# Self-attention: the output product's bias moves from a TensorE matmul to a GpSimd addition on the reloaded residual

## What is computed

```
x = x + cross_attention(layernorm(x), ctx, ctx, ...)
x = x + self_attention(layernorm(x), Wq, bq, Wk, bk, Wv, bv, Wo, bo)
x = x + experts(layernorm(x), ...)

self_attention:  q, k, v = x @ Wq.T + bq, x @ Wk.T + bk, x @ Wv.T + bv
                 q, k = rope(q), rope(k)
                 out = softmax(q k^T * scale) v
                 return out @ Wo.T + bo
```

## Time and profile before

| | |
|---|---|
| runs (median; lowest to highest) | 2096.05 us; 2095.18 to 2098.99 |
| profiled execution | 2098.95 us |
| its span, first to last instruction | 2097.2 us |
| mean granted TensorE clock | 0.992 |
| TensorE busy | 2041.1 us, 97% |
| VectorE, ScalarE, GpSimd busy | 1500.3, 1237.5, 998.9 us |
| self-attention: first normalisation, last store | 1323.7 us, 1582.9 us |

### The profile page before, as it was taken

The page is one execution under the profiler, slowest core; times in us unless marked ns, Lnnn a source line. Parts: engine busy times, 40 slices in busy tenths (PEclk is TensorE's granted clock), DMA queues, the critical chain, the costliest instruction groups (busy, mean ns, idle before and its releaser), DMA issues.

```text
span 2097.2 us, 48240 instructions
## 1 busy us (share of the span) xinstructions
PE 2041.1 (97%) x16424; PEld 1804.3 (86%) x16425; DVE 1500.3 (72%) x2690; ACT 1237.5 (59%) x3015; POOL 998.9 (48%) x835
## 2 busy tenths in 40 slices
PE   7999999999999999999999999899998999999997
PEld 6898988898899898889889988688877888888886
DVE  6667767767767767767667676799986877666665
ACT  4656666666666656656566565477773445555553
POOL 6433333333433333333343343488883334777775
PEclk9999999999999999999999999999999999999999
DMA  4000000000010010010010001255533222333332
GB/s 159 11 21 27 24 20 25 25 20 25 10 35 25 10 35 20 15 35 15 20 35 15 20 11 33 83 159 161 162 107 100 86 76 46 54 54 53 55 55 41
DMA packets 99645, 103.89 MB, mean 50 GB/s; under 512 B 10912, under 2 KB 89120, under 8 KB 99584
## 3 DMA queue, kind: packets, MB, share of 16 engines
q1 hardware_dynamic: 85952, 84.47, 12.9%
q0 software_dynamic: 13632, 18.62, 5.5%
HBM read 72.52 MB, written 30.54 MB: 49 GB/s over the span
## 4 chain that ended last, share of the span: by engine, by line
PE 75%; POOL 9%; issue 6%; DVE 4%; DMA 3%; ACT 2%; POOLq 0%; SPq 0%; DVEq 0%; ACTq 0%
PE banks L971 43%; PE banks L1077 5%; PE banks L1062 5%; PE banks L1026 4%; POOL out_dram L2505 4%; PE banks L1746 3%; POOL index L2476 3%; DMA out_dram<-r_y,index 2%; PE banks L2344 2%; POOL r_x L2469 2%; PE banks L1809 1%; PE banks L1768 1%; PE banks L1008 1%; PE banks L1825 1%; PE banks L2364 1%
## 5 line engine op out<-in xcount | busy, mean ns | idle before, releaser
L458 POOL TENSOR_TENSOR rinv<-rsum,inverse 128x4 f32<-128x4 f32 x112 | 112.9, 1008 | 482.9 <-ACT probs L593 482.9
L971 PE MATMUL banks<-ctxT_hi,qk_hi 128*128 128x256 f32 x1024 | 300.7, 294 | 0.0
L971 PE MATMUL banks<-ctxT_hi,qk_lo 128*128 128x256 f32 x1024 | 288.9, 282 | 0.0
L593 ACT ACTIVATE probs<-banks,nbias 128x256 f32<-128x256 f32 x512 | 236.8, 487 | 87.6 <-DVE nbias L736 87.6
L971 PE MATMUL banks<-ctxT_lo,qk_hi 128*128 128x256 f32 x1024 | 288.2, 281 | 0.0
L600 ACT ACTIVATE pc<-banks 128x512 f32<-128x512 f32 x256 | 155.7, 609 | 223.3 <-PE banks L971 223.3
L685 DVE TENSOR_TENSOR pT_lo<-banks,pT_hi 128x512 fp32r<-128x512 f32 x256 | 164.7, 685 | 111.3 <-ACT pT_hi L543 110.6
L731 DVE TENSOR_REDUCE peak<-banks 128x4 f32<-128x1024 f32 x128 | 156.6, 1224 | 122.4 <-PE banks L971 122.4
L461 POOL TENSOR_TENSOR probs<-probs,rinv 128x1024 f32<-128x1024 f32 x112 | 212.3, 1896 | 20.0 <-POOL rinv L458 20.0
L971 PE MATMUL banks<-pT_hi,ctx_hi 128*128 128x512 f32 x512 | 207.5, 405 | 3.2 <-DVE pT_lo L685 1.7
L971 PE MATMUL banks<-pT_hi,ctx_lo 128*128 128x512 f32 x512 | 202.0, 394 | 0.0
(11 more groups left out here) (282 smaller groups left out, 6106.2 us busy)
## 6 DMA issues: line engine op xcount, KB each, us to landing
ctx_raw<-in_ctx_dram SPq DMA_DIRECT2D x64, 256.0 KB, 2.7
experts_w<-in_L_ffn_We_dram SPq DMA_DIRECT2D x24, 512.0 KB, 4.0
x_in<-in_x_dram SPq DMA_DIRECT2D x16, 256.0 KB, 2.8
x_again<-in_x_dram SPq DMA_DIRECT2D x16, 256.0 KB, 2.8
x_stream<-z SPq DMA_DIRECT2D x16, 256.0 KB, 2.2
s_x<-x_stream SPq DMA_DIRECT2D x32, 128.0 KB, 3.8
s_x_again<-x_stream SPq DMA_DIRECT2D x32, 128.0 KB, 3.1
x_normalised<-s_xl SPq DMA_DIRECT2D x32, 128.0 KB, 1.7
```

Of the source, the lines that this page charges most:

```text
L458: nc.gpsimd.tensor_tensor(rinv[:, s % 2, :], rsum[:, s % 2, :], inverse[:, :], ALU.pow).then_inc(rinv_done, 1)
L593: nc.scalar.activation(probs[:, s % 2, p, :], scores[:, s % 2, p // 2, (p % 2) * SK:(p % 2 + 1) * SK], ACT.Exp, bias=nbias[:, s % 2, p:p + ...
L971: last = nc.tensor.matmul(out, a, b, start=(n == 0), stop=(n == 3 * len(pairs) - 1))
```

## The change

- TensorE no longer issues the matmul that brings bo into y (one 128x128 by 128x256 matmul with its weight load for each of 32 tiles); the first product with Wo opens the sum instead.
- GpSimd gets a new last part of its half-step: behind the multiplication of the probabilities of tile n it waits for the reload of x1_again of tile n-1, adds the float32 bias row to it in place (128x256), and counts up the new semaphore `x1_biased`.
- VectorE's addition of x2 waits for `x1_biased` where it waited for the reload: in half-step n it adds tile n-2 and needs the count n-1, which GpSimd reaches in its half-step n-1.
- The semaphores `pool_past` and `dve_past`, which nothing waits on, become one, `past`. The number of their increments is the same.

```diff
--- before.py
+++ after.py
@@ -1339,7 +1339,7 @@
     weights_in = sem("weights_in")
     small_in = sem("small_in")
     pool_setup = sem("pool_setup")
-    pool_past = sem("pool_past")
+    past = sem("past")
     bias_hi = sem("bias_hi")
     bias_done = sem("bias_done")
     setup_T = sem("setup_T")
@@ -1365,7 +1365,7 @@
     x3T_stored = [sem(f"x3T_stored{i}") for i in range(2)]
     dve_step = sem("dve_step")
     pool_step = sem("pool_step")
-    dve_past = sem("dve_past")
+    x1_biased = sem("x1_biased")
 
     bank_turns = [Turns(lambda kind, k=k: [key for key in pair_order(kind) if bank_of(key) == k],
                         -2, NT // 2 + 1, 4, STEADY) for k in range(SRING)]
@@ -1496,7 +1496,7 @@
             which = slice(0 if first else 1, 2 if second else 1)
             nc.gpsimd.tensor_tensor(rstd[:, which], mv[:, which, 1], power[:, which], ALU.pow).then_inc(rstd_done, 1)
             pool.wait_ge(rstd_done, g.tile(s, 4))
-            pool.sem_inc(pool_past, 1)
+            pool.sem_inc(past, 1)
 
     def normalised(out, src, which):
         return nc.gpsimd.tensor_scalar(out, src, mv[:, which, 0:1], rstd[:, which:which + 1],
@@ -1521,13 +1521,17 @@
                 pool.wait_ge(xl_stored[s], 16 * g.at)
                 key, pairs_on = before(g, s, ("x3T", s))
                 wait_filled(pool, g, key, pairs_on)
-            pool.sem_inc(pool_past, 1)
+            pool.sem_inc(past, 1)
             normalised(xl[:, s, :], x2[:, s, :], 1).then_inc(l3_done, 1)
         if g.has(s, 0):
             pool.wait_ge(rinv_done, g.tile(s, 1))
             heads = probs[:, s, :].rearrange("p (h k) -> p h k", k=SQ)
             nc.gpsimd.tensor_tensor(heads, heads, rinv[:, :].unsqueeze(2).broadcast_to([P, SH, SQ]),
                                     ALU.mult).then_inc(probs_done, 1)
+        if g.has(s, -1):
+            o = (s + 1) % 2
+            pool.wait_ge(x1_reloaded[o], 16 * (g.at + s))
+            nc.gpsimd.tensor_tensor(x1_again[:, o, :], x1_again[:, o, :], biases[:, 2 * D:], ALU.add).then_inc(x1_biased, 1)
 
     def gpsimd(pool):
         for g in pair_turns(pool):
@@ -1642,7 +1646,7 @@
     def mean_of(dve, which, stats_at):
         dve.wait_ge(dve_step, stats_at)
 
-        dve.sem_inc(dve_past, 1)
+        dve.sem_inc(past, 1)
         step(nc.vector.bn_aggr(mv[:, which, :], stats[:, which, :]))
         return chain[0] + chain[1]
 
@@ -1670,7 +1674,7 @@
             if g.has(s, -4):
 
                 dve.wait_ge(x2_stored[s], 16 * g.at)
-            dve.wait_ge(x1_reloaded[s], 16 * g.at)
+            dve.wait_ge(x1_biased, g.tile(s, -1))
             bank, free = wait_filled(dve, g, ("y", s))
             nc.vector.tensor_tensor(x2[:, s, :], bank[:, 0:D], x1_again[:, s, :], ALU.add).then_inc(free, 1)
         if g.has(s, 3):
@@ -1763,9 +1767,8 @@
         if g.has(s, -2):
             wait_freed(pe, g, *before(g, s, ("o", s)))
             bank, done = bank_for(pe, g, ("y", s))
-            nc.tensor.matmul(bank[:, 0:D], share_r[:, :], bias[:, 2 * D:], start=True, stop=False)
             for m in range(DC):
-                last = nc.tensor.matmul(bank[:, 0:D], oT[:, m, :], woT[:, m, :], start=False, stop=(m == DC - 1))
+                last = nc.tensor.matmul(bank[:, 0:D], oT[:, m, :], woT[:, m, :], start=(m == 0), stop=(m == DC - 1))
             last.then_inc(done, 1)
         if g.has(s, 1):
             pe.wait_ge(turn_done, g.tile(s, 2))
```

## The result

| | before | after |
|---|---|---|
| runs beside each other, median (lowest to highest), us | 2097.23 (2095.18 to 2098.99) | 2152.56 (2151.78 to 2153.11) |
| profiled execution, its span, us | 2098.95, 2097.2 | 2152.07, 2150.3 |
| mean granted TensorE clock | 0.992 | 0.985 |

The ratio is 1.0257, 95% interval 1.0245 to 1.0269: slower by 55.3 us between the medians, 53.1 between the spans (predicted 52.2). The forecast was 2148.3 us with a range of 2139 to 2165; 2152.56 lies in it, 4.3 us above the forecast. In what follows Y is VectorE's addition of x2 (now line 1679), and the new addition on GpSimd is line 1534.

What follows compares the result with a forecast made beforehand. TensorE was taken as the self-attention's bound, VectorE close behind; the change makes a ring of waits through GpSimd. 27 half-steps add 49.8 us, with the tail 52.2; 2096.05 + 52.2 = 2148.3 us, range 2139 to 2165.

Steps and rivals of the forecast that it cites:

- The sum of the ring: Self-attention waits from Y through GpSimd's power, line 1529 and new addition back to Y: 9.12 us per half-step against 7.28.
- Even a free addition would make 8.4: Same round of waits with an addition costing nothing: still 8.4 us per half-step, the place costing more than the instruction.
- Part 1: Removing TensorE's bias matmul, 32 times 0.12 us: gives back at most 3.8 us, nothing if something else becomes the bound.
- The tail: Last self-attention half-steps: 29 to 30 +1.6 us, 30 to 31 -0.4, 31 to 32 +1.2, 32 to 33 0.
- rival 3: TensorE's clock falls in the new idle gaps; if through half of each round, TensorE bounds, 2197 us; chance 6%.
- From the spans to the medians: Whole run: the median of runs lies 2.9 us below the profiled execution, so 2151.2 becomes 2148.3 us.
- TensorE idles some 2 us in each half-step: Self-attention: TensorE's round of 7.16 us fits in 9.12, its transposes waiting until Y has read their shared bank.
- Rival 1: Same waits, dearer or disturbed GpSimd addition: 2164 us at 1.23 us each, 2175 at 1.58; chance 8%.
- Rival 2: VectorE's wait at Y is met in time, GpSimd's round 7.35 us: 2092 to 2099 us; chance 4%.
- 79% forecast: TensorE's busy share in the self-attention stage after the change, listed among the signs: 79%.
- Rival 4: The next stage takes some delay back, its weights and tables being ready: 2141 to 2145 us; chance 7%.
- The range: 8 in 10: 2139 us (addition at 0.64 us, two gaps given back) to 2165 us (addition at 1.23 us).

Runs made afterwards that it cites:

- e4: Kernel after the change with TensorE's bias matmul put back, so the bias is added twice: 2150.94 us, ratio to before 1.0254.
- e3: Kernel after the change without GpSimd's addition, VectorE waiting for the reload, output bias left out: 2095.11 us, ratio to before 0.9987.
- e1: Kernel after the change with GpSimd's addition a half-step earlier, still last in its half-step: 2100.66 us, ratio to before 1.0015.
- e2: Kernel after the change with GpSimd's addition moved ahead of the probabilities' scaling (line 1529), same half-step: 2102.09 us, ratio to before 1.0022.
- e9: e1 with VectorE's small plus-epsilon instruction written as a reduction, epsilon left out: 2097.47 us, ratio to before 0.9995.
- e8: Kernel after the change with GpSimd's addition between its power and the wait for that result: 2096.43 us, ratio to before 0.9991.
- e7: Kernel after the change with the bias added by GpSimd in the cross-attention, into a second stored stream: 2095.81 us, ratio to before 0.9991.

## Why the prediction was right, step by step

- **The sum of the ring**, which is the mechanism, held in each term: 1.71, 6.64, 0.68 and 0.08 us against 1.69, 6.64, 0.69 and 0.10. 27 half-steps took 246.16 us, predicted 246.2. The reading that decided was that of two lines of different engines in one timeline: GpSimd's line 1529 ends 0.97 us behind the start of the Y that would have to wait for what follows it.
- **"Even a free addition would make 8.4"**: 8.39 to 8.43, worked out from the kernel with eight columns.
- **Part 1 at nothing**: shown by e4; its bound of 3.8 us was twice what it is worth without the ring (e3).
- **The tail**: 29 to 30 7.84 (7.83), 31 to 32 6.22 (6.25). Two were missed. 30 to 31 took 7.25 us and not 6.30, because Y waited for y, not for GpSimd, with TensorE at its low clock (see rival 3). At the full clock GpSimd's side holds: in e4, which has the same ring and even the matmul more on TensorE, the stretch took 6.25 us, and Y waited for the addition. 32 to 33 took 5.28 and not 4.93: GpSimd's power there took 1.47 us, where the sum had used the 0.72 of the full half-steps; the kernel before has 1.47 us at this place too (1574.24). From the first Y to the last it is 272.75 us against 219.36, +53.4, and the first Y starts 0.15 us later; from the last Y to the end of the span some 0.4 are taken back.
- **From the spans to the medians.** The 52.2 us are to be compared with 53.1 between the spans. The medians lie 55.3 apart, because the profiled execution of the kernel before was 1.7 us above the median of its runs and that of the kernel after 0.5 below. The forecast took the 2.9 us between the profiled execution and the median of the first three runs over to the new kernel; that is scatter, and the 2148.3 came out low by it.
- **"TensorE idles some 2 us in each half-step"** in one piece was wrong in shape. It idles ahead of the transposes of the probabilities (0.76 us in the timeline above), as I said, but for longer ahead of the product with v (1.15 us there, for the rotation, line 1480): they too share a bank. The rotation stands behind Y on VectorE, so this was a second way in which TensorE hangs on Y, and I hadn't listed it. It cost nothing, as it ends inside the 9.12.
- **Rival 1** is out (715 to 738 ns, 32 times). **Rival 2** describes e1 and e2; its price for GpSimd's round, 7.35 us, was short of their 7.40 and 7.43, by the small instruction that it didn't know of; without that effect (e9) the round is 7.25 to 7.28. Of its range, 2092 to 2099, e9, e8 and e7 are inside; e1 is 1.7 us above and e2 3.1.
- **Rival 3, the clock.** It does fall in the half-steps: 0.83 in the window 1480 to 1490. The Ys there stay 9.1 us apart, since the slower matmuls fill the idle time; that is a part of why TensorE's busy share is 84% and not the 79% forecast: over two rounds at a granted clock of 1.00 (1376.55 to 1394.81 and the next three pairs) it is 80 to 81%, over those at 0.91 82 to 87%. Only in the tail did it cost time. From 30 to 31, TensorE in the timeline of the kernel after, and below it the window of that stretch:
```profile
1613.06 1.58 PE L1812 MATMUL banks<-ident,s_probs 128*128 128x128 f32 x8 [0.51 <-DVE s_x L1679]
...
1617.69 1.91 PE L1771 MATMUL banks<-s_woT,s_oT 128*128 128x256 f32 x4
```
```profile
1612.00:1620.00 8.00, 7.49 (x74) 6.13 (x58) 5.15 (x9) 4.67 (x12) 4.74 (x5) 0.59 0.22 68
```
The mean granted clock is 0.59, so it is at the lower of its two levels for most of the stretch. The same window and the same Y in e4:
```profile
1612.00:1620.00 8.00, 5.88 (x97) 4.97 (x97) 5.89 (x11) 6.74 (x16) 4.90 (x5) 1.00 0.21 68
```
```profile
1618.89 0.43 DVE L1679 TENSOR_TENSOR s_x<-banks,s_x_again 128x256 f32<-128x256 f32 x1 [0.87 <-POOL s_x_again L1534]
```
There the clock is 1.00 and the stretch 1.0 us shorter, so that in the profiled execution the low clock cost about 1 us. The same transposes took 1.06 us at 1477.53, at the full clock, and the same product 1.03 us in the kernel before (1566.58 in its tail). The rule of the Trainium skill (TensorE: Matmul & The Clock Gate, Part 1), that the low clock is the resting state and work lifts it, agrees with the trace as far as it goes: the clock falls in some half-steps and comes back, and the sum stays as it was.
- **Rival 4** is out: 0.4 us taken back, not 3 to 7 (2148.3 less 2145 and 2141).
- **The range.** Its own terms give 2140.8 us for the lower end (2148.3 - 2.8 - 4.7) and 2163.8 for the upper, where I wrote 2139 and 2165. The result is inside either.

What stays open: why the profile names no releaser for nine of the Ys, and why TensorE's busy share is 81% and not 79% even at the full clock.

## What to carry to other kernels

In a pipeline of half-steps a lead counts only by the clock: find the end of the last instruction ahead of the new one on its engine, and the start of the instruction that will wait, in one timeline; if the first is later, add up the ring once round and multiply by the number of rounds. Busy shares (GpSimd 48%) say nothing of that. A good place for a short operation is where its engine waits for itself, as in the 0.38 us behind the power, if what the operation takes beyond that fits in the engine's other idle time; and the gain on offer (here 2 us, by a kernel that leaves the work out) is worth measuring before a place is looked for.

## What the runs showed of the hardware

- VectorE's tensor with a scalar of 128 x 2 goes from 0.17 to as much as 0.73 us beside a two-input addition on GpSimd and ends 0.03 us behind it (e1), and to between 0.31 and 0.42 us beside a two-input multiplication, with the same end (e2); the reduction of the same size stays at 0.15 to 0.16 (e9), and the tensor with a scalar of 128 x 1 at 0.15 (tail of e1 and e2).
- Something like it is seen the other way round: beside VectorE's line 2176, with two inputs in SBUF (1627.28 to 1628.50 in the kernel after), GpSimd's power of 128 x 1 took 1.47 us; it took 0.55 to 0.57 where VectorE ran a reduction or the rotation with one input in PSUM. It is so in the kernel before too (1574.24); no run changed it, so the cause isn't shown.
- GpSimd's addition of two tensors in SBUF took 0.205 us for 8 elements in each partition, 0.40 for 128, 0.73 for 256 and 1.28 for 512.
